# A decoder layer on one core: twenty turns of the identity ahead of x, a recurrence round in another order, and the first attention round rearranged

## The reference

```python
# block 1 (E = 512 channels, N = 16 states)
x = resid * rsqrt(mean(resid * resid) + EPS) * norm_w
skip = x @ skip_w.T;  x = silu(causal_conv4(x @ in_w.T) + conv_b)
delta = softplus(x @ Wd1.T @ Wd2_w.T + Wd2_b);  Bm = x @ WB.T;  Cm = x @ WC.T
h = exp(d_l[:, :, None] * A) * h + (d_l * x_l)[:, :, None] * B_l[:, None, :]   # for each of 256 tokens
y_l = einsum('ben,bn->be', h, C_l)
y = ((y + x * W_D) * silu(skip)) @ out_w.T;  return resid + y
# block 2
Q, K, V = heads(rope(x) @ Wq.T + bq), heads(rope(ctx) @ Wk.T + bk), heads(ctx @ Wv.T + bv)
out = softmax(Q K^T / 4) V @ Wo.T + bo
# block 3: top 3 of 15 experts by softmax(x @ gate.T), gelu-gated, plus a shared gelu-gated expert
```

## Time and profile before

| | before |
|---|---|
| median of three executions | 1912.72 us |
| the profiled execution's own time | 1917.45 us |
| its span, first to last instruction | 1915.6 us |
| mean granted TensorE clock | 0.94 |
| PE busy | 1617.7 us (84%) |
| DVE busy | 1479.5 us (77%) |
| POOL busy | 1243.0 us (65%) |
| ACT busy | 1097.1 us (57%) |

### The profile page before, as it was taken

One profiled execution on the slowest core, in us unless ns is written; L12 is line 12 of the kernel. 1 busy time (PEld: TensorE's weight loads), 2 busy tenths in 40 slices (PEclk: granted clock), 3 DMA queues, 4 the chain that ended last, 5 costly groups with the idle time before them and its releaser, 6 DMA issues. The chain is left out here.

```text
span 1915.6 us, 32761 instructions
## 1 busy us (share of the span) xinstructions
PE 1617.7 (84%) x9596; PEld 1040.1 (54%) x9597; DVE 1479.5 (77%) x2444; ACT 1097.1 (57%) x2470; POOL 1243.0 (65%) x920
## 2 busy tenths in 40 slices
PE   7787877778788777884578999998999999999997
PEld 5454544445454444452246666665677555555686
DVE  6899899999999999999856888887634444444488
ACT  5777777787778777775324555554422333333325
POOL 2988888899888888988756788883411333333300
PEclk9899999999899999987679999998999999999999
DMA  8645455444545544445246665443155222222262
GB/s 228 143 102 125 110 133 132 99 105 98 121 111 133 133 116 106 98 103 138 63 111 158 187 178 165 147 141 95 60 196 207 85 85 85 85 85 85 73 264 88
DMA packets 179287, 238.30 MB, mean 124 GB/s; under 512 B 24715, under 2 KB 115726, under 8 KB 177071
## 3 DMA queue, kind: packets, MB, share of 16 engines
q1 hardware_dynamic: 160606, 200.64, 40.6%
q0 software_dynamic: 9888, 27.80, 4.1%
q10 hardware_dynamic: 8656, 8.18, 1.5%
HBM read 172.15 MB, written 65.90 MB: 124 GB/s over the span
## 5 line engine op out<-in xcount | busy, mean ns | idle before, releaser
L709 DVE TENSOR_TENSOR_SCAN ps_h<-ps_h,inject 128x1024 f32<-128x1024 f32 x160 | 365.8, 2287 | 24.5 <-ACT ps_h L540 24.5
L370 POOL TENSOR_TENSOR inject<-common,bc_n 128x2048 f32<-128x2048 f32 x63 | 285.4, 4542 | 86.3 <-issue 65.4
L370 POOL TENSOR_TENSOR inject<-dx_n,bc_n 128x2048 f32<-128x2048 f32 x64 | 290.1, 4545 | 0.0
L540 ACT ACTIVATE ps_h<-delta_n,a_neg 128x256 f32<-128x256 f32 x512 | 213.1, 462 | 64.0 <-DVE hc L722 44.3
L1522 ACT ACTIVATE expT<-ps_t 128x512 f32<-128x512 f32 x256 | 148.8, 595 | 175.8 <-PE ps_t L2025 174.3
L540 ACT ACTIVATE ps_h<-common,a_neg 128x256 f32<-128x256 f32 x512 | 211.9, 463 | 45.2 <-DVE hc L722 35.1
L1673 DVE TENSOR_REDUCE neg_max<-ps_s 128x2 f32<-128x512 f32 x256 | 173.0, 680 | 83.1 <-PE ps_s L2014 80.9
L379 POOL TENSOR_TENSOR h_pool<-h_pool,bc_n 128x1024 f32<-128x1024 f32 x96 | 226.5, 2360 | 0.0
L709 DVE TENSOR_TENSOR_SCAN h_pool<-ps_h,inject 128x1024 f32<-128x1024 f32 x96 | 218.6, 2277 | 7.1 <-ACT ps_h L540 4.3
L2679 PE MATMUL ps_uh<-arena,s_xT 128*128 x440 | 210.3, 601 | 5.0 <-issue 4.9
L2383 POOL DMA_INDIRECT token_results<-common,e_y_row x82 | 80.1, 976 | 189.1 <-DVE common L2532 189.1
(11 more groups left out here) (338 smaller groups left out, 3523.7 us busy)
## 6 DMA issues: line engine op xcount, KB each, us to landing
common<-dup_rows SPq DMA_DIRECT2D x120, 256.0 KB, 6.0
bc_n<-bc_rows SPq DMA_DIRECT2D x64, 256.0 KB, 4.6
delta_n<-dup_rows SPq DMA_DIRECT2D x64, 256.0 KB, 4.6
dx_n<-dup_rows SPq DMA_DIRECT2D x64, 256.0 KB, 7.6
arena<-slot_rows SPq DMA_DIRECT2D x110, 136.0 KB, 2.1
arena<-token_results SPq DMA_DIRECT2D x8, 1536.0 KB, 18.5
dup_rows<-delta SPq DMA_DIRECT2D x32, 256.0 KB, 4.3
dup_rows<-dx SPq DMA_DIRECT2D x32, 256.0 KB, 4.5
```

Of the source, the lines that this page charges most:

```text
L370: nc.gpsimd.tensor_tensor(inject[:, at:at + 2, :, :], dx_n[c // 2][:, None, :, c % 2, :].to_broadcast([P, 2, JB, L]), bc_n[b % 2][:, 0, nq ...
L540: last = nc.scalar.activation(ps_h[k % 2][:, j, :], delta_n[c // 2][:, j, c % 2, :], ACT.Exp, scale=a_neg[:, c, nq, j:j + 1])
L709: nc.vector.tensor_tensor_scan(out.rearrange("p j t -> p (j t)"), ps_h[k % 2][:, :, :].rearrange("p j t -> p (j t)"), inject[:, k % RING, ...
```

## The change

The hunks in the order of the program (of the lines between them some context is left out):

```diff
@@ recurrence phase, SP, at the end
-            stack(qk.Qs, 0, qk.q_dram, Q_ORDER)
+            for c in range(DC):
+                stack(qk.Qs, c, qk.q_dram, Q_ORDER)
             save_q(1)
@@ recurrence phase, ACT, round loop
                 if front and i in (5, 7):
                     softplus_exp(b + 1, (i - 5) // 2)
+                if front and i == 8:
+                    take_delta(b + 1, 0)
                 if front and i in (6, 8):
                     softplus_log(b + 1, (i - 6) // 2)
                 if tail and i == 7:
                     layernorm_root(b - 1)
-                if front and i in (8, 10):
-                    take_delta(b + 1, (i - 8) // 2)
+                if front and i == 10:
+                    take_delta(b + 1, 1)
@@ recurrence phase, DVE
-            rows = (residual, row_stats, row_mean, row_var, None, square_root, newton, row_scale, row_shift)
+            rows = {4: (residual, row_stats), 5: (row_mean,), 6: (row_var,), 10: (square_root,), 11: (newton,),
+                    12: (row_scale,), 13: (row_shift,)}
...
-                if b > 0 and 5 <= i < 14 and rows[i - 5] is not None:
-                    rows[i - 5](b - 1)
+                if b > 0:
+                    for step in rows.get(i, ()):
+                        step(b - 1)
@@ recurrence phase, PE
+            for n in range(20):
+                nc.tensor.transpose(ps_h[0][:, 0, 0:P], ident[:, :], ident[:, :])
             transposes(0)
...
+                if tail and i == 2:
+                    project_out(b - 1)
                 sums(b, i)
                 if front and i in (0, 1):
                     conv(b + 1, i + 1)
                 if front and i == 1:
                     conv(b + 1, 3)
-                if tail and i == 3:
-                    project_out(b - 1)
@@ attention phase, SP
-            stack_q(0, 1)
             sp.wait_ge(pads_set, PADS)
@@ attention phase, ACT, round loop
-                    if real(b - 2) and h == 12:
+                    if real(b - 2) and h == 13:
                         take_x2T(b - 2)
@@ attention phase, DVE
+            q_chain = Chain(v, pads_set, PADS, 4)
+
+            def split_q(b, step):
+                if step == 0:
+                    v.wait_ge(q_made, b + 1)
+                    if b >= 1:
+                        v.wait_ge(q_saved, 16 * b)
+                if step < PARTS - 1:
+                    q_chain.link(nc.vector.tensor_copy(q_parts[:, :, step, :], QT[:, :, :]))
+                    q_chain.link(nc.vector.tensor_tensor(QT[:, :, :], QT[:, :, :], q_parts[:, :, step, :], ALU.subtract))
+                else:
+                    q_chain.close()
+                    nc.vector.tensor_copy(q_parts[:, :, step, :], QT[:, :, :]).then_inc(q_split, 1)
...
                     if b == 0 and h == 4:
-                        split_q(2)
-                    if b == 0 and h == 5:
                         v.wait_ge(late_got, LATE)
                         take_v(0)
+                    if b == 0 and 4 <= h < 4 + PARTS:
+                        split_q(2, h - 4)
```

More of the change, by code:

```diff
@@ L830, in _ @@
                 split(q_rows[n], q_parts[n], 18 + 4 * (AHEAD + n), qk.q_split)
-            for step in rows:
-                if step is not None:
+            for steps in rows.values():
+                for step in steps:
                     step(B - 1)
@@ L1654, in set_pads @@
                 nc.vector.memset(X[:, :, D + NE:XW], 0.0).then_inc(pads_set, 1)
-            def split_q(b):
-                v.wait_ge(q_made, b + 1)
-                if b >= 1:
-                    v.wait_ge(q_saved, 16 * b)
-                chain = Chain(v, pads_set, PADS, 4)
-                chain.link(nc.vector.tensor_copy(q_parts[:, :, 0, :], QT[:, :, :]))
-                chain.link(nc.vector.tensor_tensor(QT[:, :, :], QT[:, :, :], q_parts[:, :, 0, :], ALU.subtract))
-                chain.link(nc.vector.tensor_copy(q_parts[:, :, 1, :], QT[:, :, :]))
-                chain.link(nc.vector.tensor_tensor(QT[:, :, :], QT[:, :, :], q_parts[:, :, 1, :], ALU.subtract))
-                chain.close()
-                nc.vector.tensor_copy(q_parts[:, :, 2, :], QT[:, :, :]).then_inc(q_split, 1)
+            q_chain = Chain(v, pads_set, PADS, 4)
[10 more added lines that the diff above has]
+                    nc.vector.tensor_copy(q_parts[:, :, step, :], QT[:, :, :]).then_inc(q_split, 1)
             def row_max(b, h):
```

## The result

| | before | after |
|---|---|---|
| median | 1913.24 us (4 executions) | 1887.24 us (4 executions) |
| ratio, after to before | | 0.9852, 95% interval 0.9823 to 0.9881 |
| profiled execution: time, span | 1917.45, 1915.6 us | 1881.18, 1879.4 us |
| mean granted TensorE clock | 0.940 | 0.939 |
| busy: PE, DVE, POOL, ACT | 1617.7, 1479.5, 1243.0, 1097.1 us | 1616.6, 1479.5, 1241.9, 1094.0 us |

The kernel became 1.48% faster, 28 us by the ratio, where 41.3 were forecast (1871.4 us). The profiled execution of after is 6 us faster than the median of its own executions, that of before 4.2 us slower than its; so the two profiles stand 36.2 us apart in span, and the medians 26.0. What makes executions of one kernel differ turns out to be part of the matter of this case.

What follows compares the result with a forecast made beforehand. It took DVE to run nearly without a break in the recurrence and PE to bound attention. Terms 1.3 + 1.0 + 27.3 + 0.7 + 2.5 + 8.5 = 41.3 us off the median 1912.72 gave 1871.4 us, range 1862 to 1888.

Steps and rivals of the forecast that it cites:

- Recurrence, 27.3 and 1.0: Residual and statistics into step 4, delta ahead of the log steps: 1.95 us shorter in 14 rounds, 27.3; round 0, 1.0.
- Nothing queued behind is late: `project_db` follows that wait as before: Recurrence, PE: sums of step 2 end 3.7 us later behind `project_out`, free because PE then waits 1.47 us for POOL.
- ACT takes the place back: Recurrence: each round keeps a second wait of about 1 us for ACT or POOL, 13.3 instead of 27.3; chance 0.2.
- the slower rival: Recurrence: `project_out` at 1.2 GHz takes 6.8 us, a round loses about 3.8 us, 1952 us in all; chance 0.04.
- Twenty turns, 1.3: Start, PE: turns ahead of x raise TensorE's clock, first eight products in 1.9 us; gain 1.3 us, other end 0.
- If the twenty turns lift the clock before x comes: Start: condition under which PE saves 1.56 us on the products and 0.5 us of turns.
- The bound of 1.4 us by DVE's spare time: Start: DVE, measuring all of x, had only 1.39 us to spare before dx, so the gain is at most 1.4.
- The rival by the Trainium skill: Start: transpose-mode turns do not count as clock activity, so no gain there, the rest as forecast, 1872.7 us; chance 0.25.
- SP at the barrier, 0.7: Barrier: upper heads' six transfers go before Q's second save; barrier 2.8 us later, 3.83 of waiting gone; bounds -1 and 1.
- V before the split, 2.5: First attention round: `take_v(0)` moves earlier, PE's 5.38 us wait for V nearly vanishes; gain 2.5 us, bounds 0 and 5.35.
- `turn_x2`, 8.5: Attention: one head later, the 0.79 us wait for V goes; 0.65 in 13 rounds, 8.5 us, bounds 0 and 0.79.
- the main case's own bounds: Whole kernel: recurrence 22 to 30 us, barrier and first round 0 to 6, attention 5 to 10, so 1863 to 1883.

Runs made afterwards that it cites:

- the one with filler: The changed kernel with seven extra products a round on PE, results unused, ahead of the same two waits for POOL; ratio to before 0.9842.

## Why the prediction was right in kind and too far by 16 us

**Recurrence, 27.3 and 1.0.** The step that failed by size. The gaps closed as worked out (dx 1.13 to 0.44, the gap at step 5 gone), and a round without a slow product is 53.41 us in the profile of after, against 53.29 forecast. But the term was multiplied by 14 as if each round could be such a one. Alone these hunks give 21.4 us (18.2 to 24.5) instead of 28.3. What takes the rest is shown by the rows: `project_db` at 1.2 GHz costs 1.7 us a round, the skip product 0.3 to 0.6 in the two profiles of after (1.3 in the one with filler, 2.1 and 2.7 in before). The step "Nothing queued behind is late: `project_db` follows that wait as before" was wrong. `project_out` one step earlier made that wait 1.82 us instead of 1.47. Behind 1.45 to 1.50 us `project_db` was slow in none of 56 rounds (the profiles of before and of the four kernels that leave `project_out` where it was), behind 1.8 us in 3 of 9 and in 7 of 8 (the two profiles of after) and in 4 of 8 with the recurrence's hunks alone. The length of the wait is not shown to be the reason: with the move, some 1.9 us of small products stand between `project_out` and the wait instead of 0.6, and no run that leaves the wait unfilled changes one without the other. Such slow products stand in the profile of before too, in round 0 (`project_db`) and at the start of rounds 3 and 14 (skip product); the term was read from round 7, which has none.

**The rival "ACT takes the place back", 1885.4 us.** The time is near this rival's, and DVE's new waits do read "ACT ps_h"; yet ACT was itself waiting for PE, whose clock had fallen. Its order costs nothing beyond the 0.45 and 0.28 us: in round 12 they are all the waits that DVE has. What the prediction had in hand was the slower rival, which put 1.2 GHz into the recurrence, but at `project_out`; that product was at full speed in rounds 1 to 14.

**Twenty turns, 1.3.** Measured 0 (2.5 slower to 2.7 faster alone). They did end ahead of x, but the pause until 9.8 us was not priced: the argument "If the twenty turns lift the clock before x comes" looked at the turns and not at what PE does between them and x. In after they lifted it, and the pause gave it back. The bound of 1.4 us by DVE's spare time was wrong too, thirty turns brought dx 2.1 us ahead of before's. The rival by the Trainium skill, "TensorE: Matmul & The Clock Gate", Part 4 (PE-mode transpose), that turns don't count as activity, gave the right time for this kernel. Its time was right by luck. Thirty turns disagree with the rule, as x's turns behind them took 0.66 us instead of 1.12, and so do the last seven of the twenty in after, at 272 ns instead of 421.

**SP at the barrier, 0.7, and V before the split, 2.5.** The barrier came 3.2 us later (2.8 forecast), the first round gave 4.2 back: together 1.0 instead of 3.2 in the profiles, 1.9 (1.1 slower to 5.0 faster) measured alone. SP's term is near: 3.83 gone less 3.2 is 0.6. Mis-sized was V: of the 4.2 us that the round gives back 3.83 are the wait for the stacked Q, so some 0.4 is left for V by that estimate, not 2.5. The rows show new waits behind it, 2.54 us the largest, since scores now come before DVE has taken their predecessors' maxima between the split's steps.

**`turn_x2`, 8.5.** Right: 9.0 us alone (5.9 to 11.9), 0.76 in a regular round against 0.65.

**The sum.** Measured each alone, the parts give 21.4 + 9.0 + 1.9 + 0.0 = 32.3 us, within the interval of the whole (22.8 to 33.9); the terms don't fight each other. The range 1862 to 1888 held the time, with 0.8 us to spare, and that is luck in part: its upper end was set by the rival of ACT's order, which is not what happened, and the main case's own bounds, 1863 to 1883, did not hold it.

**Left open.** What decides in which rounds the clock falls behind PE's waits. Why some attention rounds of 23.26 us take 24.9 in other executions, where the granted clock is 1.00 (in one of the changed kernel measured again, PE waits 0.59, 0.45 and 0.94 us for DVE's row maxima); and why in the kernel with the products moved ahead dx still waits 0.7 to 1.2 us for ACT in six rounds.

## What to carry to other kernels

Where an engine's wait is shortened, look at what TensorE does ahead of each product that others wait for: in these traces a product right behind PE's wait for another engine ran at half speed in some rounds and not in others, and the wait that the profile showed was then laid to a third engine. Put such a product ahead of the wait if its operands are there; the mean clock need not rise for that to pay (0.91 against 0.93 here). A term that is multiplied by the rounds should be read from several rounds of several executions, not from the regular ones of one.

## What the runs showed of the hardware

- TensorE's clock fell to 0.50 behind a wait of PE of 1.82 us in round 7 of after, with small products (32 columns wide) ahead of it, and not behind the same wait in round 11. The falls are in other rounds in each execution.
- Of the 1.38 us that `project_db` took longer there (3.35 against 1.97), 1.26 came out as a wait of DVE, two engines further on.
- In the profile of before the granted clock reads 1.00 from 9 to 15 us, and the eight products there take 3.45 us; in that of after it reads 0.52 and they take 3.75. At the very start the durations tell the clock, not the column.
- Twenty-two and thirty-six plain f32 products of 128x128 (two records each) took 0.36 and 0.29 us each, twenty turns 0.18 to 0.23. A turn's record is 421 ns long at 1.2 GHz and 272 ns at 2.4.
- Turns lifted TensorE's clock: the last seven of twenty in after, and x's four behind thirty, took 272 ns.
- Falls of the clock need not cost time: rounds 1 to 14 are 754.45 us long at a granted clock of 0.93 in after, and 745.81 us at 0.91 with two products moved ahead of PE's waits.
- The same kernel's median differed by 1% between chips (1914.41, 1926.75, 1933.65 us for before).
